# One key block for two heads, two transposes for a half's maxima, and another order on the SyncE queue

## The reference

```python
ctx = xn @ We.T                                   # 16 context features a token
scores = Q @ K^T * DK**-0.5 + 0.1 * (ctx @ ctx^T) # 16 heads of 8
attn = softmax(scores); a = (attn @ V) @ Wo.T     # per batch
y = sum over the top 2 of 8 experts of prob * (gelu(xn @ w1 + b1) @ w2 + b2)
out = x + a + y
```

## Time and profile before

| what | value |
|---|---|
| runs, us | 708.39 median of 3 (707.06 to 710.24) |
| the profiled execution, us | 708.61, of which the span of the program is 706.9 |
| PE, DVE, ACT, POOL busy | 92%, 87%, 77%, 66% |
| granted TensorE clock, mean | 0.98 of full speed |
| PE's share of the chain that ended last | 62% |
| DVE's share of it | 20% |

### The profile page before, as it was taken

How to read it: one execution, slowest core, us unless ns; L and a number is a source line. 1 busy time by engine, 2 the same in 40 slices (tenths; PEclk the granted TensorE clock), 3 DMA queues, 4 the chain that set the end, 5 groups by cost and what they waited for, 6 DMA issues and landing times.

```text
span 706.9 us, 24553 instructions
## 1 busy us (share of the span) xinstructions
PE 648.2 (92%) x7800; PEld 431.8 (61%) x7800; DVE 614.9 (87%) x1106; ACT 541.7 (77%) x1123; POOL 467.7 (66%) x542
## 2 busy tenths in 40 slices
PE   0367799999999999989999999999999999999997
PEld 0264345555555555579999999998455555555454
DVE  8979789999899999868888888888999999999991
ACT  2583378888888888778888888888778878778775
POOL 8680468676687767226656656656687878878774
PEclk9996799999999999999999999999999999999999
DMA  9859656866766757684555554553667778677752
GB/s 246 316 159 320 166 135 170 207 166 180 198 165 178 208 167 176 164 129 100 101 106 99 108 100 100 106 101 72 154 160 189 177 189 184 170 183 192 170 121 80
DMA packets 162947, 113.32 MB, mean 160 GB/s; under 512 B 72624, under 2 KB 150448, under 8 KB 162864
## 3 DMA queue, kind: packets, MB, share of 16 engines
q1 hardware_dynamic: 153632, 90.63, 52.7%
q0 software_dynamic: 8192, 16.86, 9.7%
q10 hardware_dynamic: 1040, 4.76, 1.8%
HBM read 55.42 MB, written 47.19 MB: 145 GB/s over the span
## 4 chain that ended last, share of the span: by engine, by line
PE 62%; DVE 20%; issue 6%; SPq 5%; DMA 3%; ACT 2%; ACTq 0%; DVEq 0%
PE bank L1267 13%; PE mx L1256 13%; PE bank L1140 12%; DVE mx L960 11%; PE bank L1118 10%; PE mx L1152 6%; PE bank L1038 2%; DMA stack<-qk_dram 2%; DVE A L795 2%; DVE mT L966 2%; PE bank L1202 2%; DVE lo_qk L980 1%; ACT A L712 1%; PE bank L1169 1%; SPq L318 1%
## 5 line engine op out<-in xcount | busy, mean ns | idle before, releaser
L712 ACT ACTIVATE A<-bank 128x512 f32<-128x512 f32 x502 | 278.4, 597 | 62.9 <-PE bank L1140 53.9
L960 DVE TENSOR_REDUCE mx<-mx 128x4 f16<-128x1024 f32 x256 | 302.8, 1205 | 20.6 <-PE mx L1152 11.6
L583 POOL TENSOR_SCALAR rows<-rows,slot_p 128x128 f32<-128x128 f32 x142 | 112.1, 799 | 95.7 <-DVE rows L1015 95.6
L1140 PE MATMUL bank<-stack 113*128 113x256 f16 x1004 | 171.4, 277 | 1.4 <-ACT A L712 0.6
L569 POOL DMA_INDIRECT slots_x<-rows,pos x128 | 123.7, 966 | 53.0 <-PE bank L1140 32.6
L613 POOL DMA_INDIRECT rows<-slots_y,pos x128 | 121.4, 948 | 39.7 <-PE bank L1140 18.3
L1118 PE MATMUL bank<-A,V 128*32 128x256 f32 x2048 | 137.1, 385 | 1.3 <-ACT A L712 1.3
L756 ACT ACTIVATE rows<-mx,b 128x256 f32<-128x256 f32 x284 | 111.7, 475 | 25.5 <-PE mx L1256 23.7
L1140 PEld LDWEIGHTS bank<-stack 113*128 113x128 f16 x1004 | 72.7, 98 | 90.1 <-ACT A L712 55.0
L1007 DVE TENSOR_TENSOR rows<-rows 128x512 f16<-128x512 f32 x142 | 101.4, 715 | 25.0 <-ACT rows L760 22.5
L1267 PE MATMUL bank<-w,rows 128*128 x1704 | 106.9, 219 | 1.3 <-DVE rows L1007 1.3
(11 more groups left out here) (142 smaller groups left out, 595.2 us busy)
## 6 DMA issues: line engine op xcount, KB each, us to landing
stack<-ctx_rest SPq DMA_DIRECT2D x64, 256.0 KB
stack<-qk_dram SPq DMA_DIRECT2D x128, 96.0 KB
slots_y<-rows SPq DMA_DIRECT2D x71, 128.0 KB, 2.1
qk_dram<-hi_qk SPq DMA_DIRECT2D x64, 128.0 KB
stack<-ctx_high SPq DMA_DIRECT2D x128, 64.0 KB
slots_x<-A ACTq DMA_DIRECT2D x1, 4644.0 KB, 20.0
w_stage<-in_w SPq DMA_DIRECT2D x8, 512.0 KB
qk_dram<-lo_qk SPq DMA_DIRECT2D x64, 64.0 KB
```

Source lines behind the costliest of these rows:

```text
L583: ins = pool.tensor_scalar(ye[n % 4][:, h, :], ye[n % 4][:, h, :], slot_p[:, n // 4 % 3, n % 4, h:h + 1], None, ALU.mult)
L712: act.activation(A[:, n % NA, :, :].rearrange("p h s -> p (h s)"), scores(k, n)[:, :], ACT.Exp, scale=SCALE).then_inc(s_xp, 1)
L960: dve.tensor_reduce(mx[:, a, 8 * qt:8 * qt + 8].rearrange("q (i e w) -> q i e w", i=2, e=2)[:, :, g % 2], MX[u % 2][:, :].rearrange("q (i ...
L1140: mm = pe.matmul(scores(k, n)[:, i * S:(i + 1) * S], stack[0:SHIFT + 1, par, h, 1, c * P:(c + 1) * P], stack[0:SHIFT + 1, par, h, 0, :], s ...
```

## The change

Four groups of edits. **The stack** is `stack[P, 2, 6, 4, S]`: four blocks of query columns and two of key columns, each for four heads. Two heads of different classes share one key block, and their queries lie so that one matmul of 512 columns makes both heads' shifted scores. `load` sends fewer bytes, in six DMAs: the low context rows are split into a query part and a key part. `write` has three DMAs. **The maxima** of a half are written so that two transposes of 64 by 32 turn them, and `shift_rows` has again two DMAs, of runs of 32 elements. **The order on SP**: in a step, `write` comes first, then (second attention) the output tiles, and then the two halves' `load` and `shift_rows`. In step -1 both loads and the first shift rows stand ahead of the `context` calls 1 and 2, and `context(3)` stands in step 0. **The start**: `part_c` has memory of its own, which drops a wait of ACT; `context` sends the high features to four places instead of two; two `clear` calls of ACT take the place of three of SP; `START` is 8.

```diff
-START = 4
+START = 8
-        stack = sb("stack", [P, 2, H, 2, S], F16)
+        stack = sb("stack", [P, 2, 6, 4, S], F16)
+        part_c = sb("part_c", [P, 4, 2, 2 * S], F16)
-        mT = sb("mT", [32, 2, 2, P], F16)
+        mT = sb("mT", [64, 2, 2, 2, 32], F16)
+        def q_side(par, h):
+            return stack[:, par, h // 4, h % 4, :]
+        def k_side(par, h):
+            return stack[:, par, 4 + h // 8, h % 4, :]
+        def both_sides(row, n, par, g, i):
+            first_, second_ = 2 * g + i, 4 + g
+            return stack[row:row + n, par, first_:second_ + 1:second_ - first_, :, :]
...
             def load(half2, par2, g):
-                sp.dma_start(stack[REST:REST + 2 * DE, par2, 8 * g:8 * g + 8, :, :], rest).then_inc(s_st[par2][g], 16)
+                dst = stack[REST:REST + 2 * DE, par2, 2 * g:2 * g + 2, :, :].rearrange("r b w t -> r (b w) t")
+                sp.dma_start(dst, rest[:, :, 0:S].to_broadcast([2 * DE, 8, S])).then_inc(s_st[par2][g], 16)
+                sp.dma_start(stack[REST:REST + 2 * DE, par2, 4 + g, :, :], rest[:, :, S:2 * S].to_broadcast([2 * DE, 4, S])).then_inc(s_st[par2][g], 16)
+                high = high.rearrange("o c t -> (o c) t").unsqueeze(1).to_broadcast([DE, 2, 4 * S])
+                for i in range(2):
+                    sp.dma_start(both_sides(CROW[i], DE, par2, g, i).rearrange("r s w t -> r s (w t)"), high).then_inc(s_st[par2][g], 16)
+                sp.wait_ge(s_wr[par2], 48 * (half2 + 1))
                 for i in range(2):
                     h0 = 8 * g + 4 * i
+                    sp.dma_start(both_sides(QROW[i], 3 * DK, par2, g, i).rearrange("r s w t -> r s (w t)"), qk_dram[par2, :, :, h0 * S:(h0 + 4) * S].rearrange("s r c -> r s c")).then_inc(s_st[par2][g], 16)
...
             def write(par3, n_hq, n_lq):
-                for side in range(2):
-                    sp.dma_start(bass.AP(q.tensor, q.offset + (S if side else 2 * part), [[2 * S, P], [1, S]]), lo_qk[:, side, :]).then_inc(s_wr[par3], 16)
+                sp.dma_start(bass.AP(q.tensor, q.offset + 2 * part, [[S, P], [part, 2], [1, S]]), lo_qk[:, :, :]).then_inc(s_wr[par3], 16)
...
             def shift_rows(a, b1_, par1):
                 sp.wait_ge(s_mt, 2 * b1_ + a + 1)
-                for c in range(2):
-                    sp.dma_start(stack[SHIFT:SHIFT + 1, par1, 8 * a:8 * a + 8, 0, c * P:(c + 1) * P], mT[8 * c:8 * c + 8, par1, a, :]).then_inc(s_mr[par1][a], 16)
+                rows_ = stack[SHIFT:SHIFT + 1, par1, 2 * a:2 * a + 2, :, :].rearrange("r b w (c j i q) -> r (b w c) j i q", c=2, j=2, i=2)
+                for i in range(2):
+                    sp.dma_start(rows_[:, :, :, i, :], mT[32 * i:32 * i + H, par1, a, :, :]).then_inc(s_mr[par1][a], 16)
...
             def attend(s, f, k, first_half=True):
+                if f["p"] and k != -1:
+                    write_ahead(k, b3_, par3, half3)
+                if k == 0:
+                    context(3)
+                if not first_half and f["c"]:
+                    store_rows(s, k)
                 for g in range(2):
+                    if k == -1:
+                        if g == 0:
+                            for h in range(2):
+                                load(half2, par2, h)
+                        shift_rows(g, b1_, par1)
+                        if g == 0:
+                            write_ahead(k, b3_, par3, half3)
+                        context(g + 1)
+                        continue
                     if f["l"]:
-                        if k is None or k >= 0:
-                            sp.wait_ge(s_ex, 16 * b + 8 * g + 8)
+                        sp.wait_ge(s_ex, 16 * b + 8 * g + 8)
                         load(half2, par2, g)
                     if f["m"]:
                         shift_rows(g, b1_, par1)
-                    if g == 0 and f["p"]:
...
-                        write(par3, n_hq, n_lq)
...
+                if g in (3, 9):
+                    clear(act, 8 if g == 3 else 12, 12 if g == 3 else 16)
...
-                            for i in range(4):
-                                ins = dve.transpose(mT[:, par1, a, 32 * i:32 * i + 32], mx[32 * i:32 * i + 32, a, :])
+                            for j in range(2):
+                                ins = dve.transpose(mT[:, par1, a, j, :], mx[64 * j:64 * j + 64, a, :])
...
-                        for i in range(2):
-                            h = 8 * (g // 2) + 4 * p + 2 * (g % 2) + i
-                            mm = pe.matmul(scores(k, n)[:, i * S:(i + 1) * S], stack[0:SHIFT + 1, par, h, 1, c * P:(c + 1) * P], stack[0:SHIFT + 1, par, h, 0, :], start=True, stop=True)
-                        mm.then_inc(s_ex, 1)
+                        h, w = 8 * (g // 2), 2 * (g % 2) + p
+                        pe.matmul(scores(k, n)[:, :], k_side(par, h + w)[0:SHIFT + 1, c * P:(c + 1) * P], stack[0:SHIFT + 1, par, h // 4:h // 4 + 2, w, :], start=True, stop=True).then_inc(s_ex, 1)
```

More of the change, by code:

```diff
@@ L314, in context @@
                 for q in range(2):
-                    lo, hi = (part_c[r][:, a:a + 1, q * S:(q + 1) * S] for a in range(2))
+                    lo, hi = (part_c[:, r, a:a + 1, q * S:(q + 1) * S] for a in range(2))
                     high, rest = (c[q, 4 * r:4 * r + 4].rearrange("i c (m t) -> (i c) m t", t=S) for c in (ctx_high, ctx_rest))
-                    sp.dma_start(high, hi.to_broadcast([P, 2, S])).then_inc(s_cw[r], 16)
+                    sp.dma_start(high, hi.to_broadcast([P, 4, S])).then_inc(s_cw[r], 16)
                     sp.dma_start(rest[:, 1:3], hi.to_broadcast([P, 2, S])).then_inc(s_cw[r], 16)
@@ L379, in fetch_probs, with write_ahead @@
                 sp.dma_start(slot_p[:, m % 3, :, :].rearrange("p r s -> p (r s)").unsqueeze(2), ps[m][:, :, 0:1], allow_slow_non_contiguous=True).then_inc(s_sp[m % 3], 16)
+            def write_ahead(k, b3_, par3, half3):
+                n_hq, n_lq, n_st = (v if isinstance(v, int) else sp.to_reg(v) for v in (b3_ + 1, b3_ + 1, 96 * half3))
+                if k is None or b3_ >= 2:
+                    for h in range(2):
+                        sp.wait_ge(s_st[par3][h], n_st)
+                write(par3, n_hq, n_lq)
             def attend(s, f, k, first_half=True):
@@ L396, in attend @@
                         sp.dma_start(b2, B2.to_broadcast([P, NE * D])).then_inc(s_b2, 16)
+                    if k == -1:
+                        if g == 0:
+                            for h in range(2):
+                                load(half2, par2, h)
[4 more added lines that the diff above has]
+                        continue
+                    if k == 1 and g == 1:
+                        for r in range(1, 4):
+                            sp.wait_ge(s_cw[r], 96)
                     if f["l"]:
-                        if k is None or k >= 0:
-                            sp.wait_ge(s_ex, 16 * b + 8 * g + 8)
+                        sp.wait_ge(s_ex, 16 * b + 8 * g + 8)
                         load(half2, par2, g)
@@ L491, in _ @@
             for par in range(2):
-                pool.memset(stack[64:P, par, :, 1, :], -1.0).then_inc(s_post, 1)
+                pool.memset(stack[64:P, par, 4:6, :, :], -1.0).then_inc(s_post, 1)
                 pool.wait_ge(s_post, par + 1)
@@ L646, in context_hi @@
                 act.wait_ge(s_cx, r + 1)
-                act.activation(part_c[r][:, 1, :], bank[5][:, :], ACT.Copy, scale=CTX / WS).then_inc(s_ch, 1)
+                act.activation(part_c[:, r, 1, :], bank[5][:, :], ACT.Copy, scale=CTX / WS).then_inc(s_ch, 1)
             def normalise(g):
@@ L705, in attend @@
                             if k == 0 and n == 0:
-                                act.wait_ge(s_zero, 64)
+                                act.wait_ge(s_zero, 48)
                             if k != 0 or g >= 2:
                                 act.wait_ge(s_pv, 4 * b + g - 1)
-                            if k == 0 and n == NA // 2:
-                                for sm in s_cw:
-                                    act.wait_ge(sm, 96)
                             act.activation(A[:, n % NA, :, :].rearrange("p h s -> p (h s)"), scores(k, n)[:, :], ACT.Exp, scale=SCALE).then_inc(s_xp, 1)
@@ L781, in _ @@
             for par in range(2):
-                classes = stack[:, par].rearrange("r (a i h) s t -> r i a h s t", a=2, i=2)
+                classes = stack[:, par, 0:4].rearrange("r (a i) h t -> r i a (h t)", i=2)
                 dve.memset(classes[0:64, 1], 0.0)
-                ins = dve.memset(classes[64:P, 0, :, :, 0], 0.0)
+                ins = dve.memset(classes[64:P, 0], 0.0)
             ins.then_inc(s_fill, 1)
@@ L844, in context_lo @@
                 dve.wait_ge(s_ch, r + 1)
-                dve.scalar_tensor_tensor(out=part_c[r][:, 0, :], in0=bank[5][:, :], scalar=CTX / WS,
-                                         in1=part_c[r][:, 1, :], op0=ALU.mult, op1=ALU.subtract).then_inc(s_cl, 1)
```

(9 more changed lines are left out.)

50 lines of the change are left out of this document (14 added, 36 removed).

## The result

| | before | changed |
|---|---|---|
| median, us | 708.18 (704.94 to 710.24, 9 runs) | 717.97 (712.12 to 720.35, 9 runs) |
| ratio to before | 1 | 1.0138, 95% interval 1.0111 to 1.0164 |
| span of the profiled execution, us | 706.9 | 717.4 |

The forecast was 706.6 with a range of 697 to 715. The changed kernel is 1.4% slower: the sign of the "slower" rival, beyond its time and above the range. The profiled execution of the changed kernel, 719.17 us, lies 1.2 us above its median; that of the kernel before, 708.61, lies .4 above.

What follows compares the result with a forecast made beforehand. PE was taken as the bound, DVE close to a tie, SP's load loop just under. First attention -3.7, opening -.8, second attention +3.3, start -.3, end -.3: -1.8, span 705.1, time 706.6 us, range 697 to 715.

Steps and rivals of the forecast that it cites:

- "slower" rival: Second attention: tiles ahead of the load, transfer of 3.6, landing at 7.05, steps of 13.98 us; 714 us, chance .20.
- What bounds the kernel now: Both attentions: PE bounds, DVE close to a tie, SP's load loop a second bound just under PE; steps about 13.2 us.
- One matmul of 512: Shifted scores: one matmul of 512 columns for two of 256 saves .15 us a step, bounds 0 and .72.
- That rival: Shifted scores: a merged matmul of 512 columns costs less than .216 us; 692 us, some 684 by 131 ns; chance .02.
- Two transposes: DVE's maxima: two transposes for four, 200 ns each, save .8 us a step; only PE's .25 of waiting counts.
- First attention: Steps of the first attention: .25 us gained in each of 15, together -3.7 us, bounds 0 and -6.0.
- the start's -.3: Start: the load for step 0 goes ahead of two `context` calls; -.3 us, bounds -3 and +1.5.
- the .40 above: PE's gain a step: .25 us from waits for DVE and .15 from the merged matmul.
- The opening: Opening of the second attention: its eight transposes stand in the chain, so halving them saves .8 us, once.
- The order on SP, second attention: Tiles ahead of the load: it starts .85 late, lands at 6.55; +.3 a step over eleven steps, +3.3 us.
- Clean gain: Both attentions: the load lands in its window, so .40 us a step is gained; 696.6 us, chance .22.
- The start gains 3: Start: the load for step 0 no longer waits for contexts; 703.5 us, chance .08.

Runs made afterwards that it cites:

- b2_four_transposes: b1_order_ctx with four transposes of 32 by 32 a half again instead of two of 64 by 32; 708.16 us, ratio 1.0015 to the kernel before.
- b3_two_of_256: b1_order_ctx with each matmul of 512 columns made by two of 256 again; 702.36 us, ratio .9929 to the kernel before.
- a2_old_order: The changed kernel with SP's order inside a step as before, `write` behind half 0's load and shift rows; 703.16 us, ratio .9928 to the kernel before.
- a1_tiles_last: The changed kernel with a step's two output tiles sent after both loads again; 706.02 us, ratio .9981 to the kernel before.
- b1_order_ctx: The changed kernel with SP's order inside a step as before and context(3) at the end of step 0; 702.15 us, ratio .993 to the kernel before.
- b4_loop_later: The changed kernel with steps 18 and 19 written out, so the second attention's hardware loop begins at k=20; 716.28 us, ratio 1.0122 to the kernel before.

## Why the prediction was wrong, step by step

The forecast put the span at 705.1 us, and it was 717.4. Of the 12.3 us between them 7.0 lie in the second attention and 5.1 before batch 16; the rest nearly cancels.

**What bounds the kernel now** was half right. The load loop as a second bound just under PE is what the changed kernel fell into. But "PE and DVE are close to a tie" was read as PE's, with two waits of .13 in it; b2_four_transposes, where DVE bounds a step of 13.36, says that DVE set part of the 13.21 us of a clean step.

**One matmul of 512** was put at .15 us a step and measured at .03 at most (13.08 to 13.05, b3_two_of_256), next to the lower bound of 0. By the 131 ns of the Trainium skill's page "TensorE: Matmul & The Clock Gate" (section "Back-to-back issue gap") pieces of .54 and .22 us would have shrunk; here the measurement decides, and 512 columns cost what twice 256 do. That rival is out.

**Two transposes** cost 205 ns each, as the 200 that was taken, and save .8 us of DVE a step. What this is worth was mis-sized, since PE's own floor came sooner; the reduces, put at 0 to .05 each, grew by .007 to .019 each, .06 to .15 a step. With plain's waits gone, the two pieces of .68 became .54, but the product of `output` grew from .50 to .59 and the piece of shifted scores ahead of it from .54 to .59 (a2_old_order), so that .14 of the .28 came back in other pieces; why these grew is open. A clean step fell by .16, not .40.

**First attention**, -3.7 forecast, with the start's -.3 a sum of -4.0; +1.1 measured. The first term that failed is the .40 above. "SP is free some .5 us before the trigger, so the load still starts at +.19" held (.17 in most steps), but landings of 6.5 to 6.9 us came in five of the steps 2 to 14. The order doesn't make these by itself: a1_tiles_last has the same order here, never lands after more than 6.25 in these steps, and needs 159.2 us from batch 4 to batch 16. Before it was 160.5, in the changed kernel 160.8, so some 1.6 us of the loss belong to this one execution, and the gain without them is 1.3 us, .11 a step, where .25 were forecast. The second is the start: the load of step 0 that step 1 needs started 3.87 us late behind write and context(3), against the -.3 that was taken between bounds of -3 and +1.5; the 5 us by which batch 1 began earlier (76.4 instead of 81.4) were gone by batch 3. PE waited for that load, and behind the wait pieces of .54 took 1.03 at a granted clock of .50, as in the loop's first pass:

```profile
91.14 2.55 DMA stack<-qk_dram
...
93.73 1.03 PE mx L1173 x8
```

**The opening** was to gain .8 where the transposes stood in the chain. They left it, but the shift rows took their place: one issue of `load` took 1.39 us (500.95), the shift rows behind it landed late, and `shifted` waited for them. The chain:

```profile
500.95 1.39 SPq L347
...
502.79 0.64 SPq L371
...
503.48 2.32 DMA stack<-mT
...
505.84 0.60 PE bank L1162 x2
```

**The order on SP, second attention**, is the step that decided. Its mechanism was the right one: .85 late forecast, 1.04 measured, 2.6 us of issue against 2.71. The size failed. The landing was 6.55 in the forecast and 6.61 in the mean, but that is luck. A DMA row of the chain runs from the start of its issue: the 3.80 above begins at 601.33, where the last issue of .37 begins, and ends at the landing, 605.13. The sum added such a row, 3.1, to issue times that already held the last issue, and so counted it twice. Counted once, its own terms give 6.18, inside the 6.3 from which the loop loses time; the double count made good what the start, the issue and the transfer (3.2, not 3.1) were short of. Then PE takes up `plain(0)` at 6.76, and the rest of the step was 7.0 to 7.2, not 7.13 - .20 = 6.93, since the gain that was subtracted wasn't there. 6.76 + 7.1 makes the 13.9 measured; +.6 a step instead of +.3, 5.3 us over the nine steps 20 to 28. The other 5 us, of the loop's first pass (15.39 and 16.03 against 13.21 and 13.22), were no term at all: the forecast priced every step like the one it had read, with SP issues of .36, though a stretched issue could be seen where SP had time to hide it.

**The rivals.** "Slower, the tiles ahead of the load" has the right mechanism and place, and its step of 13.98 is near the 13.89 measured, though its parts are not: it has the load land after 7.05 by a transfer of 3.6 behind the last issue, where 6.61 and 2.9 were measured, and the rest of the step at 6.93 instead of 7.1. Its 714 us and the 5 us of the loop's first pass come to 719, near the 718 measured; that too is in part luck, since it has gains of 2.2 us outside the second attention where .3 were lost. "Clean gain" needed the old order: b1_order_ctx is at 702.15, not the 696.6 that .40 a step gave. "The start gains 3" isn't seen in the changed kernel (by the forecast's own terms it is 703.9, not 703.5).

**What the profile was to show.** Right: a late load (1.04 us, where .7 to 1.0 was said), `plain(0)` released by a load, DVE idle before reduces, transposes of .2 us. Wrong: steps of 13.1 and 13.5, which were 13.40 and 13.89; and once in the loop the shift rows, sent in step k = 22, released `shifted`, which it had named as a sign against it.

## What to carry to other kernels

Where a queue carries a transfer that must start at a signal, price everything that the change puts ahead of it against the slack of that transfer, in the steps that run code for the first time too, and add the terms that no clean step shows. A gain that is assumed on one engine may not be subtracted again from the rest of the loop before it is sure. Here the parts were worth telling apart: the two transposes give 6 us, the merged matmul next to nothing, and the order on SP cost 15.

## What the runs showed of the hardware

- Behind a wait of PE of 2.4 us the granted clock was .51 over the next 3 us, and a late load was paid twice: 1.6 us for the wait and 1.5 for the slower rest of the step. Behind 1.6 us it stayed at 1.00 in the changed kernel and fell to .66 of the next 5 us in b4_loop_later; what decides it was not tried.
- A DMA issue of .35 us on SP took 1.97 where a block of the instruction queue arrived in the same stretch. Issues of 1.39 to 1.66 us stand beside such a block in five other places of the changed kernel from 490 us on.
- A transpose of 64 by 32 takes 205 ns, one of 32 by 32 takes 200 to 201.
- The reduce of 128 x 1024 takes 1169 to 1225 ns in the kernel before, 1178 to 1229 in b1_order_ctx and 1216 to 1229 in b2_four_transposes, all in one form. What makes one short, no run shows.
- In the chain one matmul of 512 columns takes .22 us, as two of 256 do, and two take .54, as four of 256 do.
